# A decoder of two layers on one core: the written order in which two batches share the engines is replaced by another

## The reference

```
x, ctx = (8, 256, 256)
layer 0: x = norm(x + nystrom_attention(x))      # 16 heads, 64 landmarks, 6 steps of an iterative inverse
         x = norm(x + dilated_attention(x, ctx)) # 3 branches: every token, every 2nd, every 4th
         x = norm(x + ffn(x))                    # ternary weights, gelu
layer 1: x = norm(x + memory(x))                 # decayed products of the tokens with themselves
         x = norm(x + gated_attention(x, ctx))   # 8 heads, rotary embedding, two key sets of 256
         x = norm(2 * x + experts(x))            # 8 experts, the best 2 of each token
inverse: V = 0.25 * V @ (13 I - K V @ (15 I - K V @ (7 I - K V)))   # six times, per head, 64 x 64
```

## Time and profile before

| | |
|---|---|
| median of three runs | 1876.98 us |
| profiled execution, its own time | 1885.9 us |
| its span (first to last instruction) | 1883.7 us |
| busy in the span: PE, DVE, ACT, POOL | 1420.4, 1079.2, 631.2, 372.2 us |
| mean granted clock of TensorE | 0.874 of full speed |

### The profile page before, as it was taken

One profiled execution on the slowest core, in us unless ns is written; L12 is line 12 of the kernel. 1 busy time (PEld: TensorE's weight loads), 2 busy tenths in 40 slices (PEclk: granted clock), 3 DMA queues, 4 the chain that ended last, 5 costly groups with the idle time before them and its releaser, 6 DMA issues. The chain is left out here.

```text
span 1883.7 us, 46589 instructions
## 1 busy us (share of the span) xinstructions
PE 1420.4 (75%) x19740; PEld 1174.5 (62%) x19740; DVE 1079.2 (57%) x2385; ACT 631.2 (34%) x1371; POOL 372.2 (20%) x374
## 2 busy tenths in 40 slices
PE   1797885869788586978857787885432999999970
PEld 1696673559667355967735685673231888888860
DVE  4567567556756745775776586675340444444424
ACT  1312443332254334225433313543101444444420
POOL 1003132110314211031412013240315000000016
PEclk9789997969899697989969798997755999999995
DMA  7111112121111312111132111110114777766633
GB/s 265 37 45 46 36 46 68 46 90 48 46 42 46 96 51 67 45 46 36 51 95 68 48 47 46 37 33 1 60 47 171 229 234 234 224 226 224 224 93 118
DMA packets 165449, 174.80 MB, mean 93 GB/s; under 512 B 10528, under 2 KB 130208, under 8 KB 164896
## 3 DMA queue, kind: packets, MB, share of 16 engines
q1 hardware_dynamic: 154688, 154.33, 25.8%
q10 hardware_dynamic: 7520, 9.58, 1.4%
q0 software_dynamic: 3072, 8.39, 1.4%
HBM read 126.39 MB, written 45.88 MB: 91 GB/s over the span
## 5 line engine op out<-in xcount | busy, mean ns | idle before, releaser
L2096 PE MATMUL m_bank<-e_xT,e_w 128*128 128x256 bf16 x2208 | 245.4, 273 | 0.6 <-DVE e_xT L2174 0.6
L1728 POOL TENSOR_TENSOR e_parts<-e_whole,e_parts 128x512 bf16<-128x512 f32 x96 | 114.2, 1190 | 619.1 <-ACT e_parts L1722 619.1
L2096 PEld LDWEIGHTS m_bank<-e_xT,e_w 128*128 128x128 bf16 x2208 | 216.4, 98 | 26.3 <-DVE e_xT L2174 0.9
L688 PE MATMUL bank<-arena 64*64 64x80 f32 (+2 forms) x6400 | 217.0, 227 | 6.4 <-DVE arena L873 3.5
L688 PEld LDWEIGHTS bank<-arena 64*64 64x64 f32 x6400 | 212.9, 138 | 12.1 <-issue 5.2
L2187 DVE TENSOR_TENSOR e_h<-m_bank,e_silu 128x256 f32<-128x256 f32 x184 | 78.2, 425 | 201.8 <-ACT e_silu L2139 201.8
L2108 PE MATMUL m_bank<-m_xT,e_h 128*128 128x256 bf16 x1104 | 124.1, 273 | 0.0
L2108 PEld LDWEIGHTS m_bank<-m_xT,e_h 128*128 128x128 bf16 x1104 | 108.0, 98 | 12.3
L2139 ACT ACTIVATE e_silu<-m_bank 128x256 f32<-128x256 f32 x184 | 70.8, 385 | 123.7 <-PE m_bank L2096 123.7
L943 ACT COPY arena<-bank 128x320 f32<-128x320 f32 (+1 forms) x96 | 37.6, 391 | 153.3 <-PE bank L688 152.0
L1613 ACT ACTIVATE arena<-bank 128x512 f32<-128x512 f32 x128 | 66.6, 604 | 61.2 <-PE bank L1481 61.2
(11 more groups left out here) (295 smaller groups left out, 2857.1 us busy)
## 6 DMA issues: line engine op xcount, KB each, us to landing
e_w<-parts SPq DMA_DIRECT2D x92, 512.0 KB
e_whole<-E SPq DMA_DIRECT2D x96, 256.0 KB, 3.1
parts<-e_parts SPq DMA_DIRECT2D x192, 128.0 KB, 2.8
m_xT<-parts SPq DMA_DIRECT2D x46, 512.0 KB, 7.5
slots<-zeros SPq DMA_DIRECT2D x4, 1536.0 KB, 7.2
back<-e_y ACTq DMA_DIRECT2D x23, 256.0 KB, 6.5
e_x<-slots SPq DMA_DIRECT2D x22, 256.0 KB, 6.7
w_rest<-W_rest SPq DMA_DIRECT2D x1, 3584.0 KB, 25.0
```

Source lines behind the costliest of these rows:

```text
L688: last = pe.matmul(b[r, p * width:(p + 1) * width], lhs[r, 4 * g + p, :], rhs[r, 4 * g + p, :], start=True, stop=True)
L1728: pool.tensor_tensor(out=e_parts[:, j % 2, LOW], in0=e_whole[:, j % 2], in1=e_parts[:, j % 2, HIGH], op=ALU.subtract).then_inc(sem("e_low" ...
L2096: last = pe.matmul(bank[b][:, col:col + SLOTS], w[:, wp, c, f * P:(f + 1) * P], xeT[u][:, xp, c, :], start=j == 0, stop=j == len(terms) - 1)
```

## The change

The table `ORDERS` is written anew. Each engine executes the same instructions as before, with the same waits, in another order; the new table was drawn up from instruction durations that include the time in which VectorE and GpSimd share a port. No line of the generators changes. The new table is four lines shorter, so that a line number of the kernel after is lower by four than that of the same line before, from there on (L1541 after is L1545 before).

```diff
 ORDERS = {
-    "pe": """0x4 1x4 0x1 1x1 0x2 1x2 0x2 1x1 0x1 1x1 0x8 1x1 0x11 1x8 0x6 1x47 0x1 1x7 0x2 1x3 0x1 1x2 0x1 1x7 0x8 1x5 0x2 1x10 0x2
...
+    "pe": """0x2 1x2 0x1 1x2 0x1 1x1 0x1 1x2 0x2 1x2 0x1 1x1 0x1 1x8 0x1 1x6 0x8 1x5 0x18 1x24 0x12 1x7 0x2 1x32 0x1 1x7 0x9 1x2
...
```

More of the change, by code:

```diff
@@ L145 @@
[L145 to L154, removed]
@@ new lines @@
+    0x12 1x3 0x20 1x1 0x7 1x1 0x2 1x2 0x3 1x2 0x1 1x2 0x1 1x2 0x2 1x1 0x2 1x3 0x2 1x2 0x2 1x2 0x1 1x11 0x3 1x3 0x2 1x6
+    0x12 1x1 0x1 1x1 0x9 1x1 0x2 1x4 0x1 1x6 0x1 1x1 0x7 1x1 0x2 1x5 0x1 1x7 0x4 1x1 0x2 1x2 0x6 1x2 0x1 1x3 0x4 1x2 0x3
+    1x1 0x1 1x5 0x2 1x1 0x1 1x11 0x1 1x2 0x1 1x1 0x3 1x10 0x9 1x3 0x5 1x1 0x1 1x1 0x15""",
+    "dve": """0x4 1x4 0x1 1x2 0x1 1x5 0x2 1x4 0x3 1x5 0x4 1x3 0x5 1x5 0x2 1x2 0x8 1x7 0x1 1x2 0x15 1x3 0x1 1x17 0x10 1x5 0x1 1x31
+    0x9 1x2 0x2 1x1 0x8 1x1 0x2 1x1 0x16 1x1 0x3 1x1 0x1 1x3 0x1 1x7 0x1 1x10 0x21 1x10 0x5 1x1 0x1 1x1 0x2 1x1 0x2 1x2
@@ new lines @@
+    0x1 1x31 0x9 1x2 0x2 1x1 0x8 1x1 0x2 1x1 0x16 1x1 0x3 1x1 0x1 1x3 0x1 1x7 0x1 1x10 0x21 1x10 0x5 1x1 0x1 1x1 0x3 1x1
+    0x1 1x1 0x1 1x2 0x1 1x1 0x1 1x1 0x1 1x1 0x3 1x5 0x2 1x2 0x5 1x5 0x1 1x2 0x1 1x4 0x2 1x6 0x2 1x5 0x1 1x5 0x1 1x5 0x1
+    1x5 0x19 1x1 0x11 1x4 0x1 1x9 0x1 1x9 0x1 1x2 0x1 1x2 0x1 1x11 0x18 1x1 0x5 1x3 0x8 1x2 0x2 1x13 0x1 1x3 0x16 1x6 0x1
+    1x1 0x9 1x5 0x1 1x31 0x9 1x2 0x2 1x1 0x8 1x1 0x2 1x1 0x16 1x1 0x3 1x1 0x1 1x3 0x1 1x7 0x1 1x10 0x21 1x10 0x5 1x1 0x1
+    1x1 0x3 1x1 0x1 1x1 0x1 1x2 0x1 1x1 0x1 1x1 0x1 1x1 0x3 1x5 0x2 1x2 0x5 1x5 0x1 1x1 0x1 1x5 0x2 1x6 0x2 1x5 0x1 1x5
@@ new lines @@
+    0x1 1x5 0x1 1x5 0x19 1x1 0x11 1x3 0x1 1x4 0x1 1x1 0x7""",
+    "act": """0x5 1x3 0x1 1x8 0x5 1x6 0x1 1x5 0x2 1x3 0x8 1x3 0x3 1x3 0x3 2x2 0x3 2x3 1x6 0x3 1x9 0x2 2x2 0x4 2x4 0x5 2x2 0x1 1x4
+    0x4 1x14 0x1 1x2 2x2 0x5 1x1 0x5 2x4 0x5 1x2 0x1 2x2 0x1 1x1 0x1 2x2 1x4 2x2 1x5 0x1 2x4 0x2 1x1 0x7 1x2 0x2 1x1 2x2
+    1x2 0x1 1x4 2x2 1x4 0x1 1x1 0x10 1x1 0x1 1x10 2x2 1x5 2x2 1x2 0x1 1x3 0x10 2x2 1x1 0x5 1x2 0x5 1x3 2x4 1x5 2x4 0x1 2x2
+    1x1 0x1 1x5 0x4 1x7 0x5 1x7 2x2 0x6 1x2 0x7 1x1 0x7 1x3 0x3 1x2 2x2 1x7 0x2 2x2 0x3 2x2 0x6 2x2 0x1 1x4 2x2 0x1 2x2
@@ new lines @@
+    1x5 0x4 1x5 0x4 1x2 0x1 1x1 2x2 1x5 2x2 1x1 0x13 1x2 0x1 2x4 1x1 0x6 2x2 1x3 0x3 1x6 2x2 1x3 0x3 2x2 0x9 1x4 0x1 2x2
+    0x3 1x1 2x4 1x10 2x2 1x3 0x1 1x2 0x5 1x1 0x10 1x2 0x1 2x4 0x1 2x2 0x1 1x7 2x2 1x3 0x7 2x2 0x2 1x1 0x1 2x2 1x1 2x2 1x1
+    2x2 0x2 1x3 0x1 1x8 0x1 1x1 0x10 1x1 0x1 1x17 0x1 1x3 2x2 0x10 2x2 0x5 1x1 0x5 2x4 0x1 2x2""",
+    "pool": """1x2 0x2 1x1 0x1 2x7 1x2 2x1 1x1 0x3 2x4 1x2 2x2 0x2 1x1 2x1 1x1 2x1 0x2 1x2 2x1 1x3 2x1 1x1 0x6 2x2 1x1 2x1 1x3 2x4
+    0x1 2x1 0x3 2x4 1x2 2x2 1x1 0x2 2x1 0x1 2x4 1x2 0x2 2x1 1x2 2x1 0x2 1x6 0x1 2x1 0x3 2x1 0x2 2x3 1x1 2x2 1x2 2x1 1x1
@@ L192 @@
+    0x1 2x1 0x2 2x1 0x1 2x6 1x2 2x3 1x1 0x3 1x2 0x2 1x2 0x2 1x2 2x1 1x3 2x2 1x1 0x2 2x2 0x3 2x2 0x1 2x6 1x3 2x1 1x1 2x1
+    0x4 2x7 1x3 0x2 2x1 0x1 2x4 1x1 2x1 1x1 2x1 0x1 2x1 0x1 1x2 2x3 0x2 2x1 1x6 0x6 2x2 1x1 2x1 1x1 0x1 2x2 0x1""",
+    "sp": """2x2 3x2 2x49 1x3 0x3 2x6 3x1 2x6 1x2 2x12 0x2 2x39 1x1 2x2 1x1 2x4 0x2 2x18 1x2 2x6 0x2 3x1 2x33 1x1 2x6 1x1 2x6 0x2
+    2x23 1x2 2x4 0x2 3x1 2x65 1x1 2x8 0x1""",
 }
```

62 lines of the change are left out of this document (22 added, 40 removed).

## The result

Five runs of the kernel after took 1817.69 to 1830.90 us, a median of 1829.67, against 1877.33 for the kernel before in the same comparison: a ratio of 0.973, with a 95% interval of 0.970 to 0.976. One of the five runs of before took 3790.68 us, for which nothing on record gives a reason; the other four took 1873.54 to 1878.95. The forecast was 1802 with a range of 1750 to 1862, faster with a chance of 0.88.

What follows compares the result with a forecast made beforehand. Bound: PE in most of a period, and at its end the alternation between two in-phase streams. 3 x 23.0 + 7.8 - 2 = 74.8 us off 1885.9 gives 1811.1, less 8.9 for the median 1802; own range 1780 to 1828, wide 1750 to 1862.

Steps and rivals of the forecast that it cites:

- the passages: Three stretches from one period to the next, where two in-phase streams made PE and DVE alternate; 23.0 us gained in each.
- the walk: Costing of one passage step by step on the trace's clock, up to the inverse's first products, at 417.10 before.
- (a): Passage start: four products of A move behind B's first approximate scores; B starts 5 us earlier, its scores begin at 309.1.
- (b): B's scores: its exponentials set the pace beside A's maxima, with B's first L1497 and L1502 pair; 18 us, to 327.
- (c): Next, PE is full with B's products and three score groups of A: 24.6 us and 1.4 for hand-overs, to 353.
- (d): A's end is latency: 18.1 us from last division to last norm, 5.0 for landmarks, 0.4 for B's maxima; to 376.5.
- (e): B's second exponentials stand behind A's casts; B's first products begin at 384.5, 32.6 us earlier than 417.1.
- (f): Given back behind the first products: 7 us of PE work for A's front, 2.6 of PE waits as maxima meet products.
- The layers' end: The same walk without the next front: 70.4 us instead of 78.2, so 7.8 gained.
- The weights' pieces: ACT and SP carry pieces to the layers' end, three behind A's last exponentials; 2 us lost, between 0 and 8.
- The sum for the profiled pair: Three passages at 23.0 plus 7.8 at the layers' end less 2 for pieces: 74.8 us, from 1885.9 to 1811.1.
- The port sharing: Two rope instructions that read SBUF twice run longer than a PSUM maximum; avoiding the sharing alone is worth at most 15 us.

Runs made afterwards that it cites:

- values_last: Against its control: both products with the values stand behind all four score groups, in two banks; 1911.45 us, ratio 1.020 to the kernel before.
- its control: Unchanged generators, with a table in which every engine takes whichever batch's next step is ready; 1933.29 us, ratio 1.032 to the kernel before.
- pieces_before: Against the new table: the 96 weight pieces stand where the old table had them, PE and DVE unchanged; 1829.75 us, beside 1832.64 for the new table.
- passages_new: Against the old table: the new order only in the three passages between periods, from A's first ffn step to its next Nystrom step's end; 1854.84 us, ratio 0.9875.
- after_again: The new table, unchanged, run again; 1832.64 us, ratio 0.975 to the kernel before.
- unshared_before: Against the old table: GpSimd's two frequent operations that read SBUF become memsets of their outputs; 1857.16 us, ratio 0.989.
- front_behind: Against the new table: B's next Nystrom front stands behind A's last norm on every engine, as in the old order; 1903.35 us, ratio 1.015 to the kernel before.

## Why the prediction was right, and where it was not

The direction and the mechanism were right: the gain is in the passages, through B's lead, and undoing either half of it costs 20.7 and 29.5 us in the two passages that are free of waits for pieces. The size was not: 47.7 us between the medians where I had 75, so that 1829.67 lies inside my range but just above the 1780 to 1828 of the forecast itself. Of the signs that I had named, PE's idle time ahead of the approximate scores fell from 69.1 to 13.9 us, 17.3 to 3.5 a period; the clock rose from 0.61 to 0.86; the layers' last norm ends at 1281.1, where I had 1270. The first products at 385.93, where I had 385, are a hit by luck, as the sum below shows. To compare the walk with the trace of after I add the 8.8 us by which its first period ended sooner (223.84 against 232.62 at the ffn).

- **(a)** B's scores at 309.1: after has 299.37 + 8.8 = 308.2. Right.
- **(b)** 327: A's first scores at 322.02 + 8.8 = 330.8, 3.8 us late. I had priced the exponentials, but missed a bank: the third score group claims bank 4 (bank 0 in A), which holds the product with the values until DVE has divided. That is the row with 2.34 us, and values_last against its control shows that this wait costs time.
- **(c)** 353: the last sums of weights end at 353.3 + 8.8 = 362.1, after 31.3 us instead of 26. This is the step that failed. "PE is full" was too short on both sides. The work was 27.7 us and not 24.6: A has four score groups there and I counted three, the first of them ran at the low clock (2.4 us and not 1.2), and the products L577 and L568 took 9.7 us and not 9.0. And PE waited for 3.6 us in all, where I had 1.4 for hand-overs. From 332 to 353 it is busy for 18.62 of 21 us.
- **(d)** took 25.3 us instead of 23.5, **(e)** 7.3 instead of 8. So the first products came at 394.7 and not at 384.5, 22.4 us earlier than before, where I had 32.6.
- **(f)** I had 9.6 us given back. From the first products to the dilated scores it was 0.3 us in the first passage, and 1.8 and 3.2 in the others. A's front stands among B's products, and PE is busy for 52.30 of 54 us there. Two errors of about 10 us met, and it is luck that the 23.0 a passage came out as 22.3 in the first; the others brought 20.8 and 16.7.
- **The layers' end** was to gain 7.8 less 2, and lost 3.0. A stands alone there, behind B, and pays each wait in full: from the first scores to the last norm 70.6 us instead of 56.6. What the ropes gained was paid back. The weights' pieces, for which I had 2 us, cost nothing that pieces_before could show.
- **The first period's** 8.6 us were not forecast. passages_new shows that the old order can have them too; how much of them is the order stays open.

Why (f) gave back so little can be seen in the 81 us from the first products on, before and after:

```profile
417.00:498.00 81.00, 76.31 (x1780) 70.63 (x1772) 54.86 (x126) 20.43 (x46) 10.73 (x11) 0.90 0.14 42
```

```profile
386.00:467.00 81.00, 77.18 (x1855) 70.91 (x1855) 58.77 (x139) 22.20 (x50) 10.21 (x11) 0.96 0.12 35
```

After has 75 more records of PE there, with A's front among them, and yet PE is busy for only 0.9 us more, at a granted clock of 0.96 instead of 0.90. So the higher clock may have paid for A's front. No run tried that by itself.

The sum for the profiled pair was 74.8, and 68.2 came. That it came so near is luck as well: the profiled execution of before lies 8.9 us above its median and that of after 12 below. Two other profiles of the new order on PE and DVE are slower: after_again (1825.39) has 22.0, 17.4 and 13.3 us in the passages against the trace of before, pieces_before (1830.89) 18.5, 18.1 and 15.1. So such a passage is worth 17 to 18 us and not 23. In after_again the passages fall 16.3 us short of the forecast and the layers' end 8.8, and the first period and the experts' part, for which I had nothing, give 8.2 and 2.6. How much of what the passages lack is steps (b) and (c) and how much the clock, no run separates.

The port sharing was wrong in its place. I bounded it by the ropes, L1528 and L1531, and their busy time fell by 1.2 us. Five lines of TENSOR_SCALAR instructions, with one tensor as input, make 22.8 of DVE's 23.4 us: L873, L971, L764, L763, L975. The largest of them, the group in before and in after:

```profile
L873 DVE TENSOR_SCALAR arena<-arena 64x128 f32<-64x128 f32 x16 | 12.4, 774 | 0.8
```

```profile
L869 DVE TENSOR_SCALAR arena<-arena 64x128 f32<-64x128 f32 x16 | 3.5, 221 | 0.8
```

In the trace of before, DVE and then GpSimd:

```profile
154.07 3.04 DVE L873 TENSOR_SCALAR arena<-arena 64x128 f32<-64x128 f32 x2
```

```profile
153.53 1.15 POOL L1728 TENSOR_TENSOR e_parts<-e_whole,e_parts 128x512 bf16<-128x512 f32 x1 [3.59 <-ACT e_parts L1722]
154.64 1.26 POOL L1270 TENSOR_TENSOR res<-x,rows 128x512 f32<-128x512 f32 x1
155.84 0.95 POOL L1272 MEMSET arena<- 128x1024 f32 x1
156.73 0.31 POOL L1273 MEMSET arena<- 128x256 bf16 x1
```

In after the same two instructions:

```profile
147.28 0.46 DVE L869 TENSOR_SCALAR arena<-arena 64x128 f32<-64x128 f32 x2
```

They ended at 157.1 with GpSimd's chain, memsets included; after puts them where GpSimd is idle. So it goes with all 16: in before six of them took 0.69 to 2.34 us, and each ended 0.07 to 0.08 us behind an instruction of GpSimd; the other ten, with GpSimd idle, took 0.22. In after three begin 0.04 to 0.05 us ahead of a piece on GpSimd, and take 0.22 too. The Trainium skill (SBUF — State Buffer, "Who interferes with whom") says that tensor_scalar can enter a mode with two ports and then takes the pair of ports that it shares with GpSimd, and that whoever comes second is blocked for the whole of the other's instruction. The trace agrees with it, and shows more: the second of the two, begun at 154.77, was held through three instructions of GpSimd in a row. I had bounded the sharing by the instructions that read SBUF twice, and passed over this sentence. What these 22.8 us are worth in time stays open. In unshared_before the same five lines are busy for 14.1 us less, but L873 hardly (still 713 ns, as L1270 and the memsets behind it were not touched), and no kernel moved GpSimd's chain alone.

## What to carry to other kernels

When two streams share in-order engines, it is a phase between them that can pay, and here it paid as a whole: with either half of the passage undone the kernel was slower than with either whole order. Before splicing or searching an order, look at what a background stream (here the weights' pieces) does to the engine in front of it; three kernels in which ACT waited for the pieces' DMAs, 2 us at a time, were 93 to 100 us behind before the first period was over. And a median and a profile are two executions: say where each lies before their difference is explained.

## What the runs showed of the hardware

- **The granted clock differs between executions of one kernel, and the time with it.** In one session after took 1836.09 us at 0.888 and 1822.52 at 0.898, before 1885.85 at 0.875 and 1870.56 at 0.883. Drawn to 0.885 from these pairs, before would take 1866.7 and after 1840.2; a straight line through all 40 such runs of before and 11 of after on record gives 1866.7 and 1841.7. So, as an estimate, 25 to 27 of the 48 us are there at an equal clock, and the rest comes with the clock. It reaches a little beyond the clocks that either kernel had (before at most 0.884, after at least 0.888). That the clock is higher because PE stands still less is likely, but was not tried by itself.
- **In the stretches in which PE had short work between waits, the granted clock was for a good part the lower level.** The fronts one behind the other had 0.54 (front_behind, 384 to 413 us), the maxima together 0.61; with the new order the same stretches have 0.81 to 0.86.
- **A TENSOR_SCALAR of DVE in SBUF was held behind GpSimd's instructions, memsets too.** 64x128 elements took 0.22 us with GpSimd idle, and up to 2.34 us behind a chain of it.
